# Two LoRA layers on one core: the transposed blocks of x are stored in another order, and the order is mended where they are read

## What is computed

```python
# layer 0: W0 1024x1024, adapter A0[label] 1024x32, B0 1024x32, scale 0.5
x = x + (x @ W0.T + (x @ A0[label]) @ B0.T * 0.5)
# layer 1: W1 1024x1024, bias b, adapter A1[slot] 1024x16, B1[slot] 16x1024, scale 2
x = x + (x @ W1.T + b + ((x @ A1[slot]) @ B1[slot]) * 2.0)
```

## Time and profile before

| | |
|---|---|
| median of 3 runs | 294.85 us (294.45 to 294.96) |
| the profiled execution | 294.32 us |
| its span, first to last instruction | 292.6 us |
| TensorE busy | 288.8 us, 99% of the span |
| VectorE busy | 242.8 us, 83% |
| ScalarE busy | 153.9 us, 53% |
| GpSimd busy | 30.4 us, 10% |
| granted TensorE clock | 1.0 throughout |

### The profile page before, as it was taken

How to read it: one execution, slowest core, us unless ns; L and a number is a source line. 1 busy time by engine, 2 the same in 40 slices (tenths; PEclk the granted TensorE clock), 3 DMA queues, 4 the chain that set the end, 5 groups by cost and what they waited for, 6 DMA issues and landing times.

```text
span 292.6 us, 4450 instructions
## 1 busy us (share of the span) xinstructions
PE 288.8 (99%) x1337; PEld 236.0 (81%) x1337; DVE 242.8 (83%) x368; ACT 153.9 (53%) x270; POOL 30.4 (10%) x81
## 2 busy tenths in 40 slices
PE   8999999999999999999999999999999999999996
PEld 6888888888888888878878878878878878878885
DVE  3789996999999999999996897797798698695432
ACT  3685576879257537464453463373364355355120
POOL 1718100010000501000100100100100100100000
DMA  6999420800006600093268076068068159013004
GB/s 203 323 322 325 51 37 10 137 1 2 0 0 110 98 27 1 5 148 136 46 100 217 22 130 188 18 103 220 3 108 214 16 103 237 0 36 145 0 1 146
DMA packets 100803, 29.17 MB, mean 100 GB/s; under 512 B 85548, under 2 KB 93996, under 8 KB 100788
## 3 DMA queue, kind: packets, MB, share of 16 engines
q1 hardware_dynamic: 100788, 28.99, 42.7%
HBM read 20.59 MB, written 8.39 MB: 99 GB/s over the span
## 4 chain that ended last, share of the span: by engine, by line
PE 99%; ACT 0%; DVE 0%; issue 0%
PE bank L1204 94%; PE bank L1228 3%; PE bank L1450 1%; PE bank L1416 0%; ACT b_hi L468 0%; DVE y L718 0%
## 5 line engine op out<-in xcount | busy, mean ns | idle before, releaser
L1204 PE MATMUL bank<-v_hi,lhs 128*128 128x512 f32 (+1 forms) x136 | 42.5, 377 | 0.0
L1204 PE MATMUL bank<-vt_hi,s_hi 128*128 128x512 f32 x96 | 37.3, 389 | 0.0
L1204 PE MATMUL bank<-vt_lo,s_hi 128*128 128x512 f32 x96 | 37.3, 389 | 0.0
L1204 PE MATMUL bank<-vt_hi,s_lo 128*128 128x512 f32 x96 | 37.3, 389 | 0.0
L969 DVE STREAM_TRANSPOSE xt<-raw 128x512 int32<-128x512 int32 x32 | 32.4, 1076 | 1.4 <-DMA raw<-in_x 1.4
L1204 PEld LDWEIGHTS bank<-v_hi,lhs 128*128 128x128 f32 x136 | 25.1, 188 | 4.5
L468 ACT ACTIVATE lhs<-xt 128x512 fp32r<-128x512 f32 x32 | 19.6, 626 | 13.0 <-PE bank L1204 12.7
L1204 PE MATMUL bank<-v_lo,lhs 128*128 128x512 f32 (+1 forms) x68 | 25.7, 378 | 0.0
L1204 PE MATMUL bank<-vt_hi,lhs 128*128 128x512 f32 x64 | 22.1, 406 | 0.0
L718 DVE TENSOR_TENSOR lhs<-xt,lhs 128x512 fp32r<-128x512 f32 x32 | 21.7, 686 | 0.3
L434 POOL CAST ac<-c_hi 128x128 fp32r (+1 forms) x16 | 7.2, 450 | 135.5 <-PE bank L1204 98.5
(11 more groups left out here) (167 smaller groups left out, 662.6 us busy)
## 6 DMA issues: line engine op xcount, KB each, us to landing
raw<-in_x SPq DMA_DIRECT2D x32, 256.0 KB, 4.9
out<-y SPq DMA_DIRECT2D x31, 256.0 KB, 2.7
n<-in_L_cond_W SPq DMA_DIRECT2D x16, 256.0 KB, 5.3
a<-in_L_cond_W SPq DMA_DIRECT2D x16, 256.0 KB, 5.2
a_raw<-in_L_cond_lora_A SPq DMA_DIRECT2D x8, 128.0 KB, 2.4
b_raw<-in_L_cond_lora_Bs SPq DMA_DIRECT2D x16, 64.0 KB, 2.1
e_raw<-in_L_cond_lora_Bs SPq DMA_DIRECT2D x32, 32.0 KB, 1.8
a_raw<-in_L_cond_lora_As SPq DMA_DIRECT2D x8, 64.0 KB, 2.4
```

Source lines behind the costliest of these rows:

```text
L1204: return nc.tensor.matmul(ps, lhsT, rhs, start=start, stop=stop, skip_group_check=more)
```

## The change

The transpose now writes each block of 32 contiguously, so `xt` (and with it `s_sum`, whose sums are element by element) holds the rows in the order sb, s. The operations that make the high and low parts read `xt` and `s_sum` with the two indices exchanged, and write their results as before, in the order s, sb, which is contiguous. In these reads the innermost four elements are 32 elements (128 bytes) apart, and the next four start one element further. The count of instructions, their order, all waits and all DMAs stay.

```diff
+        def in_order(t):
+            return t.rearrange("p e (sb s) -> p e s sb", sb=GR)
+
+        def by_fours(t):
+            return t.rearrange("p e (s sb) -> p e s sb", sb=GR)
...
             def a_high(b, g):
                 act.wait_ge(xt_made, 4 * b + g + 1)
-                copy(quarter(lhs_hi, g), xt[:, g, :, :], a_hi_made[g])
+                copy(by_fours(quarter(lhs_hi, g)), in_order(xt[:, g, :, :]), a_hi_made[g])
 
             def s_high(b, j):
                 act.wait_ge(s_sum_made, 4 * b + j + 1)
-                copy(s_hi[:, j, :, :], s_sum[:, j, :, :], s_hi_made[j])
+                copy(by_fours(s_hi[:, j, :, :]), in_order(s_sum[:, j, :, :]), s_hi_made[j])
...
                 for n in quarters:
-                    nc.vector.transpose(xt[:, n, :, :].rearrange("p e (s sb) -> p sb e s", sb=GR).bitcast(I32),
+                    nc.vector.transpose(xt[:, n, :, :].rearrange("p e (sb s) -> p sb e s", sb=GR).bitcast(I32),
                                         rows[:, n // 2, n % 2].bitcast(I32)).then_inc(xt_made, 1)
...
             def a_low(b, g):
                 dve.wait_ge(a_hi_made[g], b + 1)
-                tt(quarter(lhs_lo, g), xt[:, g, :, :], quarter(lhs_hi, g).bitcast(F32), ALU.subtract, a_lo_made[g])
+                tt(by_fours(quarter(lhs_lo, g)), in_order(xt[:, g, :, :]), by_fours(quarter(lhs_hi, g)).bitcast(F32),
+                   ALU.subtract, a_lo_made[g])
 
             def s_low(b, j):
                 dve.wait_ge(s_hi_made[j], b + 1)
-                tt(s_lo[:, j, :, :], s_sum[:, j, :, :], s_hi[:, j, :, :].bitcast(F32), ALU.subtract, s_lo_made[j])
+                tt(by_fours(s_lo[:, j, :, :]), in_order(s_sum[:, j, :, :]), by_fours(s_hi[:, j, :, :]).bitcast(F32),
+                   ALU.subtract, s_lo_made[j])
```

## The result

The changed kernel takes 296.97 us (median of 4 runs, 296.56 to 297.27) where the kernel before takes 294.86: a ratio of 1.0073, with a 95% interval of 1.0055 to 1.0091. It is 2.1 us slower; 0.8 us slower was forecast, with a range of 294.3 to 299.9. The forecast's own range, 294.9 to 296.9, is just missed. The profiled execution's span went from 292.6 to 294.9 us.

A forecast was written before the change was run, and what follows sets the result against it. TensorE, in the chain for 99%, was taken as the bound. No loss at place 1, place 2 or in the loop and 0.8 us at place 3 gave 294.85 + 0.8 = 295.65 us, range 294.3 to 299.9.

The forecast's parts named there:

- The transposes' gain: VectorE's transposes, now written contiguously: 0.32 us gained each in a full queue, between 0 and 0.58.
- place 1: Batch 0's u_low, room 0: lateness 8r - 8 x 0.32 - 0.32 = -0.32 us, so no loss and no gain.
- place 2: Batch 1, a_low of quarter 3 ahead of u_product: 2.2 us late, room 2.64, so no loss.
- place 3: Batch 1's u_low: 1.2 us late, room 0.42, so TensorE waits 0.8 us.
- r: What a strided read adds to each VectorE subtraction a_low and s_low: 0.32 us, between 0 and 0.56.
- The copies: ScalarE's a_high and s_high, 8 per batch: 0 to 0.43 us longer each, adding 0.27 to the wait for the second s_hi.
- every element twice: Upper bound for strided reads, every element taking two steps: 0.56 us per VectorE subtraction.
- a lead of 0.15: A VectorE result has to be there 0.15 us before its TensorE matmul.
- its line for r = 0.40: With r at 0.40, a loss of 0.3 us at place 1 and 1.8 at place 3, in all 2.1.
- Free reads: Rival: strided reads free or nearly so (r up to 0.25), 294.85 us, not slower; chance 0.30.
- Two steps per element: Rival: r = 0.56 us on the strided subtractions, 5.2 us lost in all, 300.0 us; chance 0.17.
- The fourth case: Rival: the transpose doesn't get quicker; with r = 0.32, 4.65 us lost, 299.5 us; chance 0.08.

The follow-up runs named there:

- e5: Changed kernel with batches 0 and 1 made as in the kernel before (strided transpose write, contiguous reads): 294.77 us, ratio 0.9986 to the kernel before.
- e6: Batches 0 and 1 as in the changed kernel, 2 to 7 as in the kernel before: 298.36 us, ratio 1.0118 to the kernel before.
- e10: Changed kernel with the order's mending split: transpose writes with an 8-byte step, high and low parts read pairs of neighbours: 294.74 us, ratio 0.9999 to the kernel before.
- e8: Changed kernel with reads of 8-byte step in a_high and a_low, 16-byte in s_high and s_low; run once, VectorE 688 and 1080 ns, ScalarE 665 and 1129.
- e1: Changed kernel with ScalarE's copies reading contiguously, only VectorE's subtractions strided: 296.46 us, ratio 1.0054 to the kernel before.
- e3: Changed kernel with the transpose's strided write put back and the strided reads kept: 300.96 us, ratio 1.0214 to the kernel before.
- e2: Changed kernel with VectorE's subtractions reading contiguously, only ScalarE's copies strided: 294.68 us, ratio 0.9996 to the kernel before.
- e7: Contiguous transpose writes and reads, no strided access on any engine; the store's DMA puts each row at its place: 303.13 us, ratio 1.028 to the kernel before.

## Why the prediction was right, point by point

**The bound, and the stretch of the loss: right.** TensorE is full, and only VectorE's queue up to `u_low` of batch 1 is tight. e5 and e6 show that the loop is free and that the first two batches carry all. The transposes' gain was sized rightly: 1.29 us for the first four (the sums start at 89.39 for 90.68), and 1.90 us for three in a row where 1.9 was forecast.

**The places within it: only one of three.** The forecast had no loss at place 1 (batch 0's `u_low`) and place 2 (`u_product` of batch 1), and one gap of TensorE "and no other". Measured were 0.24 us at place 1, 1.0 at place 2 and 0.8 at place 3, the `u_low` of batch 1. That place 3 shows the forecast's 0.8 us is luck: `u_low` of batch 1 ended 2.74 us later than before (149.06 for 146.32), where the forecast had 1.2, and places 1 and 2 had already paid for nearly all of the difference.

**Slower, and not the same: right, with the size too small.** 2.1 us where 0.8 was forecast. The stated range holds the result because it reached up to the rivals' times; the forecast's own range ended 0.07 us below it. Two terms were mis-sized.

- *r*, 0.32, is 0.42: VectorE's eight strided subtractions before batch 0 shifted its queue by 3.37 us (`e_p` at 101.64 for 99.56, plus the 1.29). The step that failed is the carrying over of the transpose's excess by distances of starts. By durations the excess of the transpose was 1076 - 690 = 0.39 us (690 from e10), and that of a subtraction with the same 16-byte step is 1080 - 688 = 0.39 (e8): the same price. In distances a transpose is 0.92 apart, but a strided subtraction 1.0. The 128-byte step adds 0.03 to 0.05.
- *The copies*, bounded by 0.43, cost 0.55 us. The bound "every element twice" was wrong: a strided element has a price of its own, and ScalarE, quicker per element, loses more by it. That made the wait for the second `s_hi` 0.58 us rather than the 0.15 + 0.27 of the forecast.

With these the sum gives 8 x 0.42 - 8 x 0.32 - 0.32 = 0.5 us at place 1. `u_low` was 0.3 late there: two transposes that stood alone before another instruction saved 0.38 each, not 0.32, and the idle time took up 0.41. At place 2 it is 7 x 0.42 + 0.43 - 2.64 = 0.7 (1.0 measured: TensorE's matmul came 0.46 us after `a_low(3)` ended, where a lead of 0.15 was reckoned). Place 3 then has 3.36 - 1.28 + 0.43 - 0.42 = 2.1 in all, 1.4 beyond place 2's 0.7. 0.8 was measured: place 2, with the longer `u_product` behind it, had paid 0.4 more than the sum has, and the matmul came 0.06 us after `u_low`, where 0.15 was reckoned. Together 2.6, for 2.3 in the profile and 2.1 by the medians. The warning that the sum is steep in r, and that place 1 joins in from 0.36, was the useful part: its line for r = 0.40 (0.3 at place 1, 1.8 at place 3, 2.1 us in all) is close to what was measured.

**The rivals.** Free reads fell at the first look at the groups: with contiguous copies beside them strided subtractions still take 1107 and 1116 ns (e1). Two steps per element fell for VectorE (1.13, not 1.24). The fourth case was made as e3: it lost 6.2 us where the text had 4.65 with r = 0.32; with 0.42 it is 4.65 + 16 x 0.1 = 6.25. Its condition, a transpose that is slow by itself, fell with 710 ns.

## What to carry to other kernels

Read the room at each place where the bound engine waits, as a sum of one queue, rather than its share of busy time: VectorE had 17% idle time and the kernel still lost, since the 12 instructions that set `u_low` of batch 1 all ran in the full stretch. A stride that is moved from the writer to the readers is paid once per reader, here 4 strided operations for 16. And this permutation could be split so that each side keeps two neighbours in each 16 bytes, which cost next to nothing (e10): it took 11 us off VectorE, though no time off the kernel, whose bound is TensorE.

## What the runs showed of the hardware

- The price of a stride is a rate of its own, nearly the same on both engines, and not a multiple of the engine's step. An estimate of the fixed part of a duration is twice the 512-element row less the 1024-element row: 2 x 682 - 1245 = 119 ns on VectorE, 2 x 624 - 1054 = 194 on ScalarE. If the fixed part is the same with a stride, what remains per element is 1.10 ns and 0.84 contiguous; with a 16-byte step (1080 - 119) / 512 = 1.88 and (1129 - 194) / 512 = 1.83 (e8); with a 128-byte step 1.98 and 1.93 (the changed kernel).
- A strided write costs what a strided read does: 1132 and 1129 ns on ScalarE. A strided read and a strided write in one VectorE instruction cost what one does (1087 and 1080 ns).
- A step of 8 bytes, or pairs with a jump between them, is free on VectorE and costs ScalarE 0.03 to 0.04 us, for reads. A transpose's write with an 8-byte step is free as well (690 ns).
- With strided reads on ScalarE beside them, VectorE's strided subtractions take 1.13 in place of 1.11 us (e1); ScalarE's copies take 1.18 us with and without strided reads on VectorE (e2).
- Stores of 128 rows whose outermost dimension is 4 (2 KB a row, the last two 1 KB) keep the DMA engines 0.23 busy while nothing else runs, at 88 GB/s, and put 6.7 us on the end of the kernel (e7).
